# A perceiver layer on one core: where the short superstep of cross-attention stands, and how its last supersteps are cut

## The reference

```
qp = LN(x) @ wi            # wi 512 x 64;   kp = ctx @ wi;   vp = kp (the same projection)
x  = x + tile16(qp + softmax(qp kp^T / 8) vp) @ Wo + bo            # cross-attention, one head of 64, output tiled 16 times
h  = LN(x);  k, q, v = pattention(h, kK, kV), (h, qK, qV), (h, vK, vV)    # pattention: softmax(h K^T / sqrt(512)) V
x  = x + self-attention block with causal heads, pattention(pK, pV), and a pattention feed-forward (fK, fV)
x  = x + top-2 of 8 experts
```

## Time and profile before

| | before |
|---|---|
| median of 3 runs | 551.2 us (550.33 to 552.48) |
| the profiled execution | 552.37 us, its span 550.6 us |
| PE busy | 509.6 us (93%) |
| DVE busy | 419.7 us (76%) |
| ACT busy | 328.4 us (60%) |

### The profile page before, as it was taken

How to read it: one execution, slowest core, us unless ns; L and a number is a source line. 1 busy time by engine, 2 the same in 40 slices (tenths; PEclk the granted TensorE clock), 3 DMA queues, 4 the chain that set the end, 5 groups by cost and what they waited for, 6 DMA issues and landing times.

```text
span 550.6 us, 11108 instructions
## 1 busy us (share of the span) xinstructions
PE 509.6 (93%) x4215; PEld 345.9 (63%) x4215; DVE 419.7 (76%) x708; ACT 328.4 (60%) x639; POOL 34.7 (6%) x105
## 2 busy tenths in 40 slices
PE   5989999999999987689998989898799999999995
PEld 1434444444454444479866777687688888888873
DVE  2277778777877786958574876998898998998984
ACT  2445544554455445546574636876587788778772
POOL 2000001111110101000312000000000000000000
PEclk9999999999999997899999999998999999999998
DMA  8899898888987400506420302558867987986001
GB/s 332 325 347 397 303 340 323 325 320 334 377 339 265 164 1 2 202 29 230 154 78 1 141 13 80 227 197 331 311 233 280 389 318 250 364 323 210 0 2 40
DMA packets 35937, 122.45 MB, mean 222 GB/s; under 512 B 2609, under 2 KB 2609, under 8 KB 31282
## 3 DMA queue, kind: packets, MB, share of 16 engines
q1 hardware_dynamic: 35602, 121.27, 59.3%
q10 hardware_dynamic: 288, 0.52, 0.3%
HBM read 121.26 MB, written 0.52 MB: 221 GB/s over the span
## 4 chain that ended last, share of the span: by engine, by line
PE 45%; DVE 11%; ACT 4%; issue 2%; DVEq 0%; POOL 0%; ACTq 0%
PE score_banks L1053 15%; PE bank L1086 8%; PE score_banks L662 2%; PE score_banks L713 2%; DVE w_split L1832 2%; PE score_banks L862 2%; PE bank L672 1%; PE score_banks L886 1%; PE score_banks L1009 1%; PE bank L862 1%; PE bank L1062 1%; PE bank L662 1%; PE bank L536 1%; ACT w_split L1362 1%; ACT arena L1367 1%
## 5 line engine op out<-in xcount | busy, mean ns | idle before, releaser
L1132 ACT ACTIVATE xprobs<-score_banks,small 128x512 f32<-128x512 f32 (+1 forms) x104 | 67.9, 664 | 98.2 <-DVEq L1564 69.3
L1689 DVE TENSOR_TENSOR w_split<-arena,w_split 128x1024 fp32r<-128x1024 f32 x96 | 114.0, 1220 | 6.2 <-ACT w_split L1263 4.2
L1263 ACT ACTIVATE w_split<-arena 128x1024 fp32r<-128x1024 f32 x96 | 100.7, 1060 | 14.6 <-PE score_banks L1053 9.9
L490 PE MATMUL bank<-arena,wi_sb 128*64 128x512 f32 (+1 forms) x400 | 91.9, 600 | 6.4 <-DMA arena<-in_ctxT 6.4
L1053 PE MATMUL score_banks<-w_split,xg 128*128 128x512 f32 x384 | 88.9, 390 | 1.0 <-issue 1.0
L1573 DVE STREAM_TRANSPOSE xprobsT<-xprobs 128x1024 f32<-128x1024 f32 (+1 forms) x52 | 61.6, 1184 | 34.1 <-ACT xprobs L1132 32.7
L1053 PEld LDWEIGHTS score_banks<-w_split,xg 128*128 128x128 f32 x384 | 71.7, 188 | 16.9 <-ACT xg L1432 1.3
L1545 DVE TENSOR_REDUCE small<-score_banks 128x2 f32<-128x1024 f32 (+1 forms) x52 | 57.2, 1138 | 15.0 <-PE score_banks L521 15.0
L490 PEld LDWEIGHTS bank<-arena,wi_sb 128*64 128x64 f32 x400 | 26.6, 138 | 54.9 <-issue 53.6
L521 PE MATMUL score_banks<-k_full,hT 64*32 64x256 f32 (+1 forms) x1664 | 50.0, 372 | 5.3 <-ACT xprobs L1132 4.1
L536 PE MATMUL bank<-xprobsT,v_rows 128*64 128x256 f32 x392 | 48.5, 390 | 0.0
(11 more groups left out here) (303 smaller groups left out, 724.8 us busy)
## 6 DMA issues: line engine op xcount, KB each, us to landing
arena<-in_ctxT SPq DMA_DIRECT2D x23, 2048.0 KB, 8.9
arena<-in_w12T SPq DMA_DIRECT2D x32, 1024.0 KB, 5.0
arena<-in_w3T SPq DMA_DIRECT2D x16, 1024.0 KB, 5.6
arena<-in_fKT SPq DMA_DIRECT2D x4, 1024.0 KB, 8.0
arena<-in_fV SPq DMA_DIRECT2D x4, 1024.0 KB, 5.3
arena<-in_ctxT SPq DMA_DIRECT2D x4, 512.0 KB, 6.1
arena<-in_Wo SPq DMA_DIRECT2D x1, 2048.0 KB
arena<-in_kKT SPq DMA_DIRECT2D x1, 1024.0 KB, 11.0
```

Of the source, the lines that this page charges most:

```text
L490: last = pe.matmul(kp_bank[b][DH * h:DH * (h + 1), 0:half], wi_sb[:, k, :], ctx_buf[:, b, k, h * half:(h + 1) * half], start=(k == 0), sto ...
L1132: act.activation(xprobs[:, qb, 0:2 * width].rearrange("p (h n) -> p h n", h=2), score_banks[:, 2 * p:2 * p + 2, 256 * q:256 * q + width], ...
L1263: act.activation(w_split[:, i % 4, 0, :], raw, ACT.Copy).then_inc(part_high, 1)
L1689: return dve.tensor_tensor(w_split[:, i % 4, 1, :], raw, w_split[:, i % 4, 0, :].bitcast(F32), ALU.subtract)
```

## The change

The 512 remaining tokens become superstep 0, as one block, and supersteps 1 to 12 take 2048 tokens each. The first load is half as large; all chunks behind it start 512 tokens into the context. Wo is loaded behind chunk 4 and folded from superstep 2 on. The fold product, its copies and the query projections with their additions move into supersteps 10 and 11. Superstep 11 makes its value products by query tile (`pv_rows`: both parts of one tile, 128 columns wide) and takes one tile before the last keys' transposes. Superstep 12 goes by tile all the way: scores, maxima, exps, fade, value product, transposed accumulator, projection (two products into one bank in place of an addition on DVE) and norm. The row sums are summed by one product with a block matrix `quads`, made by POOL at the start. kK's split parts get a place of their own, so that they can be made before the last superstep; the square-root table is loaded ahead by a tiny ACT step.

```diff
-    HALF0 = (S - STEPS * STEP) // 2
+    SMALL = S - STEPS * STEP
+    HALF0 = SMALL // 2
...
+        kK_split = over("kK_split", flat_at + 4 * 4096, [P, 2, 2, UNIT // 2])[:]
...
-                sp.dma_start(ctx_buf[:, 0, k, :], ctx_cols[:, k, 0:STEP]).then_inc(ctx_first_in[k], 16)
+                sp.dma_start(ctx_buf[:, 0, k, 0:SMALL], ctx_cols[:, k, 0:SMALL]).then_inc(ctx_first_in[k], 16)
...
-                b, width = n % 2, STEP if n < STEPS else 2 * HALF0
+                b, at = n % 2, SMALL + (n - 1) * STEP
                 if n >= 2:
                     sp.wait_ge(kp_done, n - 1)
-                sp.dma_start(ctx_buf[:, b, :, 0:width], ctx_cols[:, :, n * STEP:n * STEP + width]).then_inc(ctx_in[b], 16)
-                if n == 5:
+                sp.dma_start(ctx_buf[:, b, :, :], ctx_cols[:, :, at:at + STEP]).then_inc(ctx_in[b], 16)
+                if n == 4:
...
+            pool.memset(quads[:], 0.0).then_inc(consts_done, 1)
+            for n in range(7):
+                pool.wait_ge(consts_done, MADE["slot_id"] + 1 + n)
+                pool.affine_select(out=quads[:], in_=quads[:], compare_op=ALU.not_equal, fill=1.0, base=32 * (n - 3),
+                                   pattern=[[-1, P]], channel_multiplier=1).then_inc(consts_done, 1)
...
-            for u in range(2, LAST + 1):
+            for u in range(2, LAST):
...
-                if 3 <= u < 3 + len(wo_sums):
-                    fold_wo(u - 3)
-
-            for g, ring, raw in halves("pK"):
+                if u < 2 + len(wo_sums):
+                    fold_wo(u - 2)
...
+            place_last_fade(0)
+            denominators(LAST, LAST % 2)
+            place_last_fade(1)
...
+            def next_keys(u, p):
+
+                pe.wait_ge(ctx_in[1 - p], 16 * u)
+                if 2 * u - 2 + p:
+                    pe.wait_ge(v_done, 2 * u - 2 + p)
+                kp(2 * u - 1 + p, 1 - p, p, HALF)
...
+            def pv_rows(u, par, st, dst):
+
+                pe.wait_ge(probs_turned, 4 * u + 2 * st + 2)
+                pe.wait_ge(v_done, 2 * u + 1)
...
+                for part in range(2):
+                    for j in range(nt):
+                        for h in range(2):
+                            block = (2 * h + part) * nt + j
+                            last = pe.matmul(dst[DH * h:DH * (h + 1), :], v_rows[par][:, part, j * P + DH * h:j * P + DH * (h + 1)],
+                                             xprobsT[par][:, 4 * st:4 * st + 4, 32 * block:32 * (block + 1)],
+                                             start=(part == 0 and j == 0), stop=(part == 1 and j == nt - 1))
+                return last
...
-            kp(0, 0, HALF, (0, 1))
...
-            kp(0, 0, HALF, (2,))
...
-            kp(0, 0, HALF, (3,))
+            kp(0, 0, 1, HALF0, (3,))
...
-            turn_keys(0, 0, 0)
-            pe.wait_ge(ctx_in[1], 16)
-            kp(1, 1, HALF)
+            turn_keys(0, 0, 0, HALF0, 1)
+            next_keys(1, 0)
             pe.wait_ge(ev("q_high"), 1)
-            scores(0, 0, 0)
-            turn_keys(0, 0, 1)
-            next_keys(1, 0)
-            scores(0, 0, 1)
+            scores(0, 0, 0, 1, HALF0)
             next_keys(1, 1)
+            scores(0, 0, 1, 1, HALF0)
             turn_keys(1, 1, 0)
             turn_keys(1, 1, 1)
-            superstep(1, 1)
-            for u in range(2, LAST - 1):
+
+            next_keys(2, 0)
+            scores(1, 1, 0)
+            pv(0, 0, 0, 1, HALF0)
+            scores(1, 1, 1)
+            next_keys(2, 1)
+            turn_keys(2, 0, 0)
+            turn_keys(2, 0, 1)
+            for u in range(2, LAST - 2):
                 superstep(u, u % 2)
 
+            scores(LAST - 2, 0, 0)
+            pe.wait_ge(ev("wo_summed"), len(wo_sums))
+            pe.wait_ge(consts_done, MADE["fold"])
+            pe.wait_ge(v_done, seen(LAST - 2, 0))
+            pe.matmul(kp_bank[0], fold[:], wo_sum, start=True, stop=True).then_inc(ev("wo_folded"), 1)
+            turn_o(LAST - 4)
+            pv(LAST - 3, 1, 0)
+            pe.wait_ge(ev("wo_dup_ready"), 2)
+            next_keys(LAST - 1, 0)
+            scores(LAST - 2, 0, 1)
+            next_keys(LAST - 1, 1)
+            pv(LAST - 3, 1, 1)
+            turn_keys(LAST - 1, 1, 0)
+            turn_keys(LAST - 1, 1, 1)
+
             scores(LAST - 1, 1, 0)
-            turn_o(LAST - 3)
-            next_keys(LAST, 0, HALF0)
-            pv(LAST - 2, 0, 0)
-            scores(LAST - 1, 1, 1)
-            pe.wait_ge(ev("wo_summed"), 7)
-            pe.wait_ge(consts_done, MADE["fold"])
-            pe.wait_ge(v_done, 2 * LAST)
...
             for st in range(ST):
                 pe.matmul(kp_bank[st], q_full[0:DH + 1, st * P:(st + 1) * P], wo_ext, start=True,
                           stop=True).then_inc(ev("xattn_ready"), 1)
+            turn_o(LAST - 3)
+            pv(LAST - 2, 0, 0)
+            pv(LAST - 2, 0, 1)
+            scores(LAST - 1, 1, 1)
+            pe.wait_ge(ev("q_added"), 1)
+            next_keys(LAST, 0)
+            turn_o(LAST - 2)
+            pe.wait_ge(ev("q_added"), 2)
+            next_keys(LAST, 1)
+            pv_rows(LAST - 1, 1, 0, of_bank[:, 0:P])
+            turn_keys(LAST, 0, 0)
+            turn_keys(LAST, 0, 1)
+
+            scores(LAST, 0, 0)
+            pv_rows(LAST - 1, 1, 1, of_bank[:, P:T]).then_inc(o_ready, 1)
             turn_o(LAST - 1)
-            pv(LAST, 0, 0, 1, HALF0)
-            pe.wait_ge(ev("acc_faded"), 1)
-            for st in range(ST):
-                last = pe.transpose(turned_bank[:, T + st * P:T + (st + 1) * P], acc[:, st, :], ident[:])
-            last.then_inc(ev("acc_turned"), 1)
-            pe.wait_ge(ev("o_total"), 1)
-            for st in range(ST):
-                pe.matmul(SB[2 + st], o_sb[:, st * P:(st + 1) * P], wo_dup, start=True, stop=True).then_inc(ev("xattn_ready"), 1)
...
+            def turn_acc(st):
+
+                pe.wait_ge(ev("acc_faded"), st + 1)
+                if st:
+                    pe.wait_ge(ev("acc_out"), st)
+                pe.transpose(turned_bank[:, T + st * P:T + (st + 1) * P], acc[:, st, :], ident[:]).then_inc(ev("acc_turned"), 1)
...
+
+                cols = slice(st * P, (st + 1) * P)
+                pe.wait_ge(o_out, LAST + 1 + st)
+                pe.matmul(bk, o_sb[:, cols], wo_dup, start=True, stop=False)
+                pe.wait_ge(ev("acc_out"), st + 1)
+                pe.matmul(bk, acc_T[:, cols], wo_dup, start=False, stop=True).then_inc(ev("xattn_ready"), 1)
+
+            pv_rows(LAST, 0, 0, of_bank[:, 0:P]).then_inc(o_ready, 1)
+            turn_acc(0)
+            project(0, kp_bank[1])
+            keep_awake(kp_bank[0], 8)
+            pe.wait_ge(denom_done, LAST + 1)
+            pe.wait_ge(consts_done, MADE["quads"])
+            pe.matmul(SB[1][:, 0:QB], quads[:], denom, start=True, stop=True).then_inc(ev("denom_summed"), 1)
+            pv_rows(LAST, 0, 1, kp_bank[0][:, 0:P]).then_inc(o_ready, 1)
+            turn_acc(1)
+            project(1, SB[3])
...
-            keys_out(0, 0, 1)
-            values_out(0, 0, 1)
-            soft(0, 0, 0)
+            act.wait_ge(keys_turned, 1)
+            act.activation(v_rows[0][:, 0, 0:HALF0], kp_bank[1][:, 0:HALF0], ACT.Copy).then_inc(v_done, 1)
             keys_out(1, 1, 0)
-            soft(0, 0, 1, (0,))
+            soft(0, 0, 0, width=HALF0 // 4)
             keys_out(1, 1, 1)
-            soft(0, 0, 1, (1,))
+            soft(0, 0, 1, width=HALF0 // 4)
...
-
-            soft(LAST - 1, 1, 0)
-            keys_out(LAST, 0, 0, HALF0)
-            soft(LAST - 1, 1, 1)
-            fade_out(LAST - 1)
-            act.wait_ge(ev("wo_folded"), 1)
-            act.activation(wo_dup, kp_bank[1], ACT.Copy).then_inc(ev("wo_dup_ready"), 1)
-            act.activation(wo_ext[0:DH, :], kp_bank[1][0:DH, :], ACT.Copy).then_inc(ev("wo_dup_ready"), 1)
-            o_copy(LAST - 2)
...
                 at = SPLIT_UNITS.index(unit)
+                if unit == "kK":
+                    act.wait_ge(kp_done, 2 * LAST + 1)
+                elif unit == "qK":
+                    act.wait_ge(o_ready, LAST + 2)
...
+            act.wait_ge(ev("wo_folded"), 1)
+            act.activation(wo_dup, kp_bank[0], ACT.Copy).then_inc(ev("wo_dup_ready"), 1)
+            act.activation(wo_ext[0:DH, :], kp_bank[0][0:DH, :], ACT.Copy).then_inc(ev("wo_dup_ready"), 1)
+            superstep(LAST - 2, 0)
+
+            soft(LAST - 1, 1, 0)
+            o_copy(LAST - 2)
+            soft(LAST - 1, 1, 1, (0,))
+            keys_out(LAST, 0, 0)
+            soft(LAST - 1, 1, 1, (1,))
+            fade_out(LAST - 1)
+            keys_out(LAST, 0, 1)
+            attn_high("kK", 0, 1)
+            values_out(LAST, 0, 0)
+            values_out(LAST, 0, 1)
+            attn_high("kK", 1, 2)
...
+            def last_o(st, bk):
+
+                cols = slice(st * P, (st + 1) * P)
...
+                act.activation(o_sb[:, cols], bk, ACT.Copy).then_inc(o_out, 1)
```

(77 more changed lines are left out.)

## The result

| | before | after |
|---|---|---|
| median | 551.84 us (550.33 to 552.49, 4 runs) | 557.33 us (556.61 to 558.52, 4 runs) |
| the profiled execution, its span | 552.37, 550.6 us | 556.61, 554.9 us |

A forecast was written before the change was run, and what follows sets the result against it. TensorE and the DVE and ACT loop were both taken as full, leaving only start and tail. Start -5.95, fold +1.15, projections +5.2, tail 0, clock +1.7: +2.1 us, so 553.3 us; own range 551.5 to 555, wide 546.5 to 558.

The forecast's parts named there:

- The start: Up to superstep 2's scores or first maximum: 5.95 us earlier from the small first superstep, before any clock loss.
- The clock: TensorE's granted clock falling behind idle stretches at the start: 0 to 3.4 us, with the middle, 1.7, taken.
- Chunk 2's landing: Context chunk at the start, issued after kp 0 ends at 10.9, flowing from about 13: landed with receipt at 18.4.
- The last supersteps: Fold product moved into superstep 10, +1.15 us; query projections and value products in superstep 11, +5.2.
- By-tile value products: Value products in matmuls of 128 columns instead of 256: 1.75 us taken, bounds 1.7 to 3.4, weight loads hidden.
- The tail: From superstep 12's scores to the mark: change 0, a longer softmax chain traded for key scores at full clock.
- the kK wait: Ahead of the last superstep's first maximum, DVE's second kK subtraction waits for ACT's copy: about 2 us lost.
- the mark: Start of the second tile's key scores, 239.12 before; a shift there is a shift of the end; put at 239.5.
- Rival B: Slower: clock falls at 225 to 227, slowing tile 1's value product, transposes and projection: 556.6 us, chance 0.23.
- Rival C: No change: the sum without a clock loss, +0.4 us: 551.6 us, chance 0.22.
- Rival A: Faster: start limited by PE alone (-7.7), no hold by kK halves, no clock lost: 547.8 us, chance 0.26.
- From profile to medians: Whole kernel: profiled execution would take 554.5 us, taken as 1.2 above the median of the runs, giving 553.3.

The follow-up runs named there:

- e1: Changed kernel with four products of constants on TensorE in each of its two idle stretches at the start: 555.53 us, ratio 1.0096.
- e10: Changed kernel with the small first chunk in a free arena slot, so the third chunk's load needn't wait for its key products: 555.01 us, ratio 1.0066.
- e8: Changed kernel with tile 0's last value product, accumulator transpose and projection held back until tile 1's exps are transposed: 565.56 us, ratio 1.0276.
- e3: Changed kernel with the second half of kK subtracted after the last softmax instead of ahead of the last superstep's first maximum: 556.44 us, ratio 1.009.
- r0: The changed kernel run again, unchanged, in the second group of runs: 558.01 us, ratio 1.0131 to the kernel before.
- e5: Changed kernel with e2's and e3's edits and without the eight keep_awake products ahead of tile 0's transposes: 547.86 us, ratio 0.9925.
- e2: Changed kernel with superstep 1's scores moved ahead of the next key products at the start: 549.83 us, ratio 0.9983.

## Why the prediction was wrong

The walk held from point to point; two of its terms were too small, both at the start. The start came to -2.08 and not the -4.25 of the sum, outside even the bounds given for it (-7.7 to -3; with the 3.4 named for the clock the upper one should have been -2.55).

- **The clock** (forecast: "I take the middle, 1.7"). It cost 2.8: 26.17 and 26.18 us between the same two points with two falls, 23.36 without (e1), and the walk's own figure, 21.9 to 45.2, was 23.3. The step that failed is pricing one fall at half its longest length, where two idle stretches had been counted. There were two falls. By e10, which had only the second, that one cost 0.8 and the first 2.0, if the two add up (24.13 less 23.36, 26.17 less 24.13). The products behind the gaps ran 4.9 us longer in all, of which 2.8 shows on the path. The Trainium skill (TensorE: Matmul & The Clock Gate, HAM oscillation — how this bites in real kernels) has idle gaps throttling the array again. The trace of after agrees at both gaps, but e10 and e8 have the first gap at the same length (2.85) and no fall behind it. The wait for the third chunk shows the same: a fall behind 2.11 us of it in e3, none behind 2.98 in r0 or 3.09 in e5. So the length of one gap decides nothing by itself. What decides stays open.
- **Chunk 2's landing** (forecast: 18.4). The key products that need it start at 19.32 in one profile of after and 20.64 in the other. I had kp 0 done at 10.9, the chunk flowing from about 13 and at the full 401 GB/s from there; no row of before showed the 13. In the first profile kp 0 ended 0.8 later (its last four products stand at 10.97, with a length of 0.75), and the transfers ran slowly for 1.5 us before they were at full rate (the last number is GB/s):

```profile
12.00:13.50 1.50, 1.50 (x16) 0.86 (x12) 0.00 (x0) 0.16 (x1) 0.00 (x0) 1.00 0.53 93
14.50:18.00 3.50, 3.50 (x59) 1.26 (x58) 0.00 (x0) 1.97 (x4) 0.00 (x0) 1.00 1.03 424
```

That kp 0 stands in the load's path is shown by e10 (18.23 without). It isn't the whole of it: in r0 kp 0 ended at 10.86, as walked, and the products still began only at 20.64. Why that load took longer isn't known.

Together 1.0 + 1.1 = 2.1 us at superstep 2's scores in the profile of after (49.07 against 46.9), 3.5 in r0.

- **The last supersteps** (+6.35) came to +5.85, the fold with its 1.13 us and the query projections included.
- **By-tile value products** (1.75 net): 1.92 and 1.97 for 32 products of 128 columns, against 1.90 for 16 of 256. The trace agrees with what the prediction took from the Trainium skill (TensorE: Matmul & The Clock Gate, Step-by-step: what each phase is for): the 32 weight loads took 1.73 us and lay beside the products' 1.97.
- **The tail** (0): -0.05. This isn't luck of opposite errors: with the 3.34 us by which scores 12 are late (211.94 for 208.6), the kK wait, the scores of tile 1, the held transposes, the key scores in 3.02 and the mark itself (239.5 + 3.34 = 242.84) stand within 0.3 us of where they were put. The clock fell at the scores of tile 1 (3.29 for 1.96) as said, and none of its "0 to 0.5" is to be seen at the mark.
- **Rival B** (the clock falls at 225 to 227) did not come, though its 556.6 is the number nearest to the 557.33 measured; that is chance. The granted clock was 1.00 from 223.5 to 234, tile 1's value product took 1.97, its projections 1.13 and 1.02. Tile 0's projection and the products of constants fill PE from 225.6 to 229.0, and the denominators' product stands at 229.82. **Rival C** (no clock lost) is refuted by e1. **Rival A** is refuted for the kernel as it is; but a start as early as its own is there for one line moved (e2: 41.58, below even the -7.7 bound of 43.4, which took the order of scores and key products as given).
- **From profile to medians.** The profiled execution of after was to take 554.5 and took 556.61: 2.1 of the 4.0 us of error lie there: 2.2 from the start, +0.6 from behind the mark and -0.5 from the last supersteps, rounded. The other 1.9 come from the step to the median: I took a profiled execution to lie 1.2 above it, as before, and this one lay 0.7 below. Between two executions of the same kernel r0 shows a landing of the chunk 1.3 us later; what else makes the spread of single executions wasn't measured.

## What to carry to other kernels

When the smallest block is moved to the front, the engines behind it have little to cover waits with: write out the order there so that what feeds the slowest loop (here the scores) stands ahead of anything that waits for another engine. A buffer that the first block shares with a later load turns that block's compute into part of the load's latency. Count idle stretches that a change adds to TensorE as candidates for a lower clock, price every one of them (not the middle of one) with the products behind it on the path, and look again at fills of constants after a change: the same eight held up one kernel and were too few in the other.

## What the hardware did unexpectedly

The stretch behind the mark is the same in after and in all experiments on it, yet from the mark to the end it took 309.9 us (e2), 310.9 (e10), 312.1 (after), 313.6 (e5) and 314.0 (e3), and 311.0 in e5's own repetition. Windows of the same 60 us of e2 and of e5, counted from the mark (the number third from the end is the granted clock):

```profile
356.39:376.39 20.00, 18.75 (x105) 15.89 (x104) 17.49 (x43) 13.91 (x19) 0.00 (x0) 1.00 0.71 273
376.39:396.39 20.00, 15.78 (x80) 12.77 (x80) 17.93 (x33) 13.59 (x18) 0.00 (x0) 1.00 0.82 294
396.39:416.39 20.00, 20.00 (x100) 16.71 (x99) 18.51 (x25) 15.15 (x19) 0.00 (x0) 1.00 0.82 313
```

```profile
354.09:374.09 20.00, 19.21 (x100) 16.85 (x98) 17.15 (x41) 13.89 (x19) 0.00 (x0) 0.91 0.71 271
374.09:394.09 20.00, 15.79 (x76) 13.07 (x76) 16.89 (x34) 12.04 (x15) 0.00 (x0) 0.93 0.79 292
394.09:414.09 20.00, 20.00 (x83) 16.17 (x82) 17.72 (x23) 14.48 (x17) 0.00 (x0) 0.90 0.70 246
```

The same work ran once at a granted clock of 1.00 throughout and once with falls in all three windows. From the mark to the end the two profiles differ by 3.7 us, as much as the change moved the mark. The clock isn't all of it: e3 took 314.0 with falls in two of these windows only (0.90 and 0.93). The profiles of before and of after have almost the same falls there (0.91, 0.94, 0.97 and 0.91, 0.94, 0.98), so they don't disturb the comparison of these two. But one profile of each kernel can't say where 2 us went unless the same stretches are compared, as at the mark here.
